# Layer 0 of a two-layer block: normalised rows kept on chip and stored with their routing weights, and slots found as 64 rows by 32 tiles

## The chip, the cores and the metric

The kernel runs on one core of a Trainium2 chip. Its engines are TensorE (PE in the rows; PEld is its weight load), VectorE (DVE), ScalarE (ACT), GpSimd (POOL) and SyncE (SP), which issues most of the DMAs. The metric is the device time of one execution in microseconds; lower is better.

## The reference, cut to what matters

The input is `x` of 16 sequences, 256 tokens, 128 channels: 4096 tokens, 32 tiles of 128. Two layers follow one another, each an attention and a mixture of experts that both read the same normalised rows. Only layer 0 is changed:

```python
xn = layernorm(x)                                   # no weights
q, v, k = split(xn @ Wqvk)                          # 16 heads of 8
w  = softmax(mask(q @ k.T) / sqrt(128))
at = (w @ v) @ Wo
logits = xn @ router_w.T + router_b                 # 8 experts
top_vals, top_ids = top_k(logits, 2); p = softmax(top_vals)
for e in range(8):                                  # capacity 2048 slots: 256 for each expert
    tok, slot = nonzero(top_ids == e, size=256)
    y = (a * (b * sigmoid(b))) @ W_out[e]           # a = xn[tok] @ W[e], b = xn[tok] @ V[e]
    out[tok] += y * p[tok, slot]
x = x + at + out
```

Here the capacity is 2 * 512 * 2 / 8 = 256, computed from a batch of 2, so that most of the 8192 choices get no slot; a token gets at most two slots.

## The kernel before, in words

Each engine has its own program, and semaphores (`wait_ge`, `then_inc`) join them; the order of work is the order in which each engine's function is written. There is no scheduler.

**First stage (0 to 70 us).** For each sequence b, `normalise0` (ACT) writes normalised rows into `xn_ring` (4 buffers), `transposes0` and `products0` (PE) make q, k and v, and q and k are split into three bf16 parts, in `parts0` (ACT), `rest0` (DVE), `middle_parts` and `low0` (POOL). `keep_parts` (SP) stores these to DRAM as `qk_parts` (two DMAs, L436 of 64 KB and L438 of 512 KB), from a ring `qk_p` of 4 buffers, and `load_half` (L451) brings them back stacked as `q_st` and `k_st`, rows by head. `keep_xn` (L456) stores the normalised rows, 128 KB for a sequence, in `x_rows`; the experts gather from there later. At the end SP waits until all parts are stored (L481), and only then moves the first row maxima (`move_max`, L486) into `q_st`.

**The 64 groups (70 to 343 us).** A group is 4 heads of one sequence. In `slot(g)` every engine does its part for group g and its neighbours: PE makes the scores of group g + 3 for the maxima and those of group g again, transposed (`scores`), DVE takes row maxima of group g + 2 (`row_max_late` L1221, `row_max_early` L1214), PE turns them (L1649), ACT negates them, SP moves them, ACT takes the exponential of group g (L874), POOL cuts it off above the diagonal (`cut_off`, L683), PE multiplies with v (`weigh`), and DVE divides (`divide`, L1307 and L1309). The buffer `probs` of the exponentials lies over the first stage's `qk_p` and `xn_ring`.

**Routing, woven into the slots.** In slots 0 to 4 the two best experts are found (`mark_best`, `pick_first`, `weigh_best`, `choose`). At slot `COUNT` = 5 matmuls count what is ahead of each choice. `weigh_experts` (slot 7) computes the two weights and splits them into three bf16 parts; POOL's `place_choices` runs in slot 6; `index_in` (slot 8) makes `row` and `tile_of` of each of the 64 x 128 choices. `mark_tiles` (DVE, slot 9, L1154) writes `in_tile`, and POOL's ten calls (L655, slots 10 to 19) multiply it by token numbers and weights into `of_tile`. `mark_rows` (L1160) compares 128 places with a row, 64 times, in slots 9 to 19, into `of_row`, which lies in `y_top`. `find_slots` (slot 20, L1763) is 64 matmuls of `of_row` by `of_tile` into 128 rows by 5 x 16 columns: token number and weight of each slot. `index_out` makes the indices, POOL gathers the rows in slots 24 to 31 (`collect`, L671, 16 indirect DMAs of 128 rows), and after slot 31 the experts run (`middle`), whose results go back in slots 32 to 39 (`give_back`).

## Time and profile before

| | us |
|---|---|
| median of 3 executions | 843.76 |
| lowest, highest | 843.05, 848.58 |
| the profiled execution, its own time | 841.65 |
| its span | 839.9 |
| first stage, until the first exponential | 70.47 |
| groups 0 to 19 (exponential of 0 to that of 20) | 83.57 |

All rows below are of the profiled execution, whose own time is 2.1 us under the median; its span leaves 1.75 us of it out. The three executions differ by 0.7 us but for one, which lies 5 us higher.

### The profile page before, as it was taken

The numbers are of one execution on the slowest core, as the hardware profiler recorded it, in microseconds if no ns is written. First come the engines' busy times: TensorE is split into PE (matmuls) and PEld (weight loads), VectorE is DVE, ScalarE is ACT, GpSimd is POOL, SyncE is SP. The second block draws the span as 40 slices with busy tenths as digits, with TensorE's granted clock in tenths as the row PEclk, the third lists the DMA queues.
The fourth block names the chain that finished last, engine by engine and source line by source line (L and its number), as shares of the span: only waits on it lengthen the run. The fifth ranks groups of instructions, "written<-read, shape, count | busy, mean of one in ns | idle before, by whom it ended". The sixth has DMA issues, their size and how long they took to land.

```text
span 839.9 us, 17776 instructions
## 1 busy us (share of the span) xinstructions
PE 729.9 (87%) x6148; PEld 539.8 (64%) x6148; DVE 560.2 (67%) x1107; ACT 417.8 (50%) x797; POOL 314.0 (37%) x408
## 2 busy tenths in 40 slices
PE   4658767858977999687889699999999999999997
PEld 3533434525844555486666478888888888888886
DVE  5857888734534888476898477666666666656665
ACT  5634445535434777684767344444444444444442
POOL 2663555452132577401768537121212121211211
PEclk9986899989987999998999899999999999999999
DMA  5993454122011443100112063121212121111100
GB/s 186 274 265 122 143 171 145 54 62 70 15 42 54 139 123 115 52 1 14 53 52 63 27 168 79 51 63 50 59 41 62 50 62 40 65 45 62 51 14 12
DMA packets 66083, 67.58 MB, mean 80 GB/s; under 512 B 6880, under 2 KB 44256, under 8 KB 66016
## 3 DMA queue, kind: packets, MB, share of 16 engines
q1 hardware_dynamic: 64272, 64.32, 25.8%
q0 software_dynamic: 1024, 2.10, 0.9%
q8 instruction: 42, 0.69, 0.3%
q10 hardware_dynamic: 720, 0.27, 0.1%
q14 instruction: 25, 0.20, 0.1%
HBM read 47.51 MB, written 19.01 MB: 79 GB/s over the span
## 4 chain that ended last, share of the span: by engine, by line
PE 67%; DVE 9%; issue 6%; POOL 6%; ACT 5%; DMA 3%; another core or an unknown queue 2%; SPq 1%; ACTq 0%; POOLq 0%; DVEq 0%
PE ps L1741 23%; PE ps L1966 21%; PE ps L1854 3%; DVE m L1221 2%; PE ps L1666 2%; DMA qk_parts<-qk_p 2%; ACT probs L874 2%; POOL probs L683 2%; PE ps L1559 2%; POOL x L666 2%; DVE y_top L1160 1%; PE ps L1809 1%; PE ps L1875 1%; PE ps L1577 1%
## 5 line engine op out<-in xcount | busy, mean ns | idle before, releaser
L1441 DVE SCALAR_TENSOR_TENSOR f_l<-ps,f_h 128x512 fp32r<-128x512 f32 x256 | 176.1, 691 | 114.5 <-ACT f_h L956 113.3
L956 ACT ACTIVATE f_h<-ps 128x512 fp32r<-128x512 f32 x256 | 153.0, 598 | 197.4 <-PE ps L1741 197.4
L1741 PE MATMUL ps<-x_hl,w_h 128*128 (+1 forms) x512 | 201.3, 393 | 0.0
L782 POOL TENSOR_TENSOR acc<-acc,yt 128x512 f32<-128x512 f32 x55 | 70.9, 1289 | 249.8 <-DVE yt L1479 249.8
L874 ACT ACTIVATE probs<-ps 128x1536 f32<-128x1536 f32 x64 | 92.9, 1451 | 47.9 <-PE ps L1586 40.3
L1741 PEld LDWEIGHTS ps<-x_hl,w_h 128*128 128x128 f32 x512 | 96.7, 189 | 19.7
L1741 PE MATMUL ps<-x_hl,w_l 128*128 (+1 forms) x256 | 100.1, 391 | 0.0
L1966 PE MATMUL ps<-f_l,w_h 128*128 128x512 f32 x256 | 99.8, 390 | 0.3 <-DVE f_l L1441 0.3
L1966 PE MATMUL ps<-f_h,w_h 128*128 128x512 f32 x256 | 100.0, 391 | 0.0
L1966 PE MATMUL ps<-f_h,w_l 128*128 128x512 f32 x256 | 99.8, 390 | 0.0
L1221 DVE TENSOR_REDUCE m<-ps 128x4 f32<-128x1024 f32 x64 | 78.1, 1220 | 19.6 <-PE ps L1577 18.0
L683 POOL TENSOR_SCALAR_AFFINE_SELECT probs<-probs 128x512 f32<-128x512 f32 x96 | 59.3, 642 | 71.4 <-ACT probs L874 71.4
L842 ACT ACTIVATE m_neg<-ps 8x128 bf16<-8x128 f32 x64 | 17.1, 267 | 77.5 <-PE ps L1649 60.7
L1966 PEld LDWEIGHTS ps<-f_l,w_h 128*128 128x128 f32 x256 | 48.1, 188 | 11.0 <-DVE f_l L1441 1.0
L1966 PEld LDWEIGHTS ps<-f_h,w_l 128*128 128x128 f32 x256 | 48.2, 188 | 10.0
L1966 PEld LDWEIGHTS ps<-f_h,w_h 128*128 128x128 f32 x256 | 48.2, 188 | 10.0
L1741 PEld LDWEIGHTS ps<-x_hl,w_l 128*128 128x128 f32 x256 | 48.4, 189 | 9.6
L1573 PE MATMUL ps<-k_st,q_st 48*128 48x128 bf16 x256 | 38.1, 233 | 14.7 <-remote 12.5
L1559 PE MATMUL ps<-mask_qk,ident_h 128*128 128x256 bf16 x128 | 28.0, 305 | 25.9 <-DVE m L1221 19.4
L1307 DVE RECIPROCAL rden<-ps 128x8 f32<-128x8 f32 x64 | 13.3, 208 | 55.5 <-PE ps L1774 33.8
L1214 DVE TENSOR_REDUCE m<-ps 128x4 f32<-128x512 f32 x64 | 43.6, 681 | 5.2 <-remote 2.8
L1666 PE MATMUL ps<-probs,v_ring 128*16 128x256 f32 x512 | 43.9, 416 | 1.0 <-ACT wvn L854 1.0
(230 smaller groups left out, 1415.8 us busy)
## 6 DMA issues: line engine op xcount, KB each, us to landing
gate_b<-gate_rows SPq DMA_DIRECT2D x64, 256.0 KB, 3.2
qk_parts<-qk_p SPq DMA_DIRECT2D x16, 512.0 KB, 3.8
k_st<-qk_parts SPq DMA_DIRECT2D x64, 96.0 KB
q_st<-qk_parts SPq DMA_DIRECT2D x64, 96.0 KB
y_tok<-zero SPq DMA_DIRECT2D x8, 512.0 KB, 3.0
w_raw<-in_w_e SPq DMA_DIRECT2D x16, 256.0 KB, 2.8
x_rows<-xn_ring SPq DMA_DIRECT2D x16, 128.0 KB, 3.4
w_up<-in_w_up SPq DMA_DIRECT2D x8, 256.0 KB, 2.8
```

The costliest lines, as they stand in the source:

```text
L683: nc.gpsimd.affine_select(tiles, tiles, pattern=[[0, GH], [1, P]], compare_op=ALU.is_ge, fill=0.0, base=0, channel_multiplier=-1)\
L782: nc.gpsimd.tensor_tensor(acc[:, :], acc[:, :], yt[:, e % 2, :], ALU.add).then_inc(summed, 1)
L874: nc.scalar.activation(probs[:, at(g, HELD), :, :], ps[:, 3:6, :], ACT.Exp, scale=float(D) ** -0.5)\
L956: nc.scalar.activation(r32(f_h[:, m % 4, :]), ps[:, m % 4, :], ACT.Relu).then_inc(f_hi, 1)
L1214: nc.vector.tensor_reduce(m8[:, at(g, 2), :, 0], ps[:, first, :].rearrange("p (h k) -> p h k", h=GH), AX.X, ALU.max).then_inc(early_max, 1)
L1221: nc.vector.tensor_reduce(m8[:, at(g, 2), :, 1], ps[:, first + 1:first + 3, :].rearrange("p c (h k) -> p (c h) k", h=2), AX.X, ALU.max).th ...
L1441: nc.vector.scalar_tensor_tensor(out=r32(f_l[:, m % 4, :]), in0=ps[:, m % 4, :], scalar=0.0, in1=f_h[:, m % 4, :], op0=ALU.max, op1=ALU.su ...
L1559: nc.tensor.matmul(scores_at(g)(c).rearrange("p (h k) -> p h k", h=2)[:, :, P:S], ident_h[:, :], mask_qk[:, :].unsqueeze(1).broadcast_to([ ...
L1573: return nc.tensor.matmul(scores_at(g)(0)[:, h * P:(h + 1) * P], qs[:, 0:P], ks[:, 0:P], start=False, stop=True, skip_group_check=True)
L1666: nc.tensor.matmul(ps_o[32 * h:32 * h + 2 * HD0, :], v_ring[:, u, 0, k * GH + h, :], probs[:, at(g, HELD), 1 + h // 2, h % 2 * S:(h % 2 + ...
L1741: last = nc.tensor.matmul(dst, r32(lhs[i]), r32(rhs[j]), start=(k == 0), stop=(k == 2))
L1966: last = nc.tensor.matmul(ps[:, 4 + e % 2, :], r32(w[i]), r32(fs[:, m % 4, :]), start=(c == 0 and k == 0), stop=(c == FC - 1 and k == 2))
```

## The change

The rows are normalised into `xn_rows`, which holds all 32 tiles with two more columns each (`XW` = 130), in place of the ring, and takes the place of `y_more`. `weigh_experts` writes the two weights of a token into these columns, in slot 6; `keep_xn` then stores the rows in slots 9 to 16, in 8 DMAs of 260 KB; the clears of `y_tok` move from slots 10 to 17 to 17 to 24. The gathered row brings both weights, and `take_weights` (DVE, in `middle`) picks one by `which`. So the bf16 split of the weights and their six POOL calls fall away.

A slot's place is now 64 rows by 32 tiles: `of_row` is made by 8 instructions of 8 x 64 columns, `in_tile` has 2048 columns, POOL makes `of_tile` in 4 calls of 1024 elements (slots 10 to 13), `find_slots` multiplies 64 columns by 64, and its result is taken in two halves. Routing runs a slot earlier (`COUNT` = 4), and `place_choices` is parted over slots 5 and 6.

In the first stage SP holds back the third and fourth part of `x` until the four weights are in; `rb0` moves to SP's queue; ACT loads its table for the square root ahead of the first moments; PE's loop over sequences is written out. PE starts the first scores when sequence 14 is through instead of 15, SP moves the first maxima without waiting for the stores, and ACT waits for the stores ahead of the first exponential.

```diff
@@ -39,7 +39,7 @@
-COUNT = 5
+COUNT = 4
@@ -51,6 +51,10 @@
+SLOT_ROWS = 64
+SLOT_TILES = SLOTS // SLOT_ROWS
+XW = D + 2
+LATE_IN = 12
...
@@ -134,15 +138,17 @@
-        found = sb("found", [P, 5, ST], where=era)
-        pick_p = sb("pick_p", [P, 2, NT], where=era)
-        r_rest = sb("r_rest", [P, 2 * NT], where=era)
-        p_parts = sb("p_parts", [P, 3, 2 * NT], BF16, where=era)
+        found = sb("found", [P, 2, ST], where=era)
+        which = sb("which", [P, 2, ST], where=era)
+        p_both = sb("p_both", [P, 2, ST], where=era)
...
-        y_more = sb("y_more", [P, NT, D], where=era)
-        xg = y_more[:, 0:ST, :]
-        xgT = y_more[:, ST:NT, :].rearrange("p t c -> p (t c)")
-        y_sb = xg
+        xn_rows = sb("xn_rows", [P, NT, XW], where=era)
+        xn_flat = xn_rows.rearrange("p t c -> p (t c)")
+        pick_p = xn_rows[:, :, D:XW].rearrange("p t c -> p c t")
+        y_more = xn_flat[:, 0:NT * D].rearrange("p (t c) -> p t c", c=D)
+        xg = xn_rows[:, 0:ST, :]
+        xgT = xn_flat[:, ST * XW:ST * XW + SLOTS]
+        y_sb = y_more[:, 0:ST, :]
...
@@ -423,9 +423,11 @@
         def _(sp):
             for c, part_in in enumerate(x_in):
+                if c == 2:
+                    sp.wait_ge(w_in, 4 * 16)
...
-            for dst, name in ((tables[:, :, :], "tables"), (rank_e[:, :, :], "rank_e"), (places[:, :], "places"), (w_o[:, :], "w_o"),
+            for dst, name in ((rb0[:, :], "rb0"), (tables[:, :, :], "tables"), (rank_e[:, :, :], "rank_e"), (places[:, :], "places"), (w_o[:, :], "w_o"),
@@ -437,6 +439,10 @@
+            def wait_stored(b):
...
+                sp.wait_ge(qk_stored[b % 4], 32 * (b // 4 + 2))
@@ -450,17 +456,15 @@
-            def keep_xn(b, v):
...
-                sp.wait_ge(xn_ready, (b + 1) * TB)
-                sp.dma_start(x_rows[ds(b * S, S)].rearrange("(t p) d -> p t d", p=P), xn_ring[:, v, :, :]).then_inc(kept[v], 16)
+            def keep_xn(k):
...
+                some = NT // 8
+                sp.dma_start(x_rows[ds(k * some * P, some * P)].rearrange("(t p) d -> p t d", p=P), xn_rows[:, k * some:(k + 1) * some, :])\
+                  .then_inc(rows_out, 16)
...
             for u in range(2):
...
-            for b in range(3):
-                keep_xn(b, b)
@@ -468,17 +472,13 @@
             def keep0(b, v):
-                if more(b, 3):
-                    keep_xn(b + 3, (v + 3) % 4)
...
                 for n in range(16):
                     if STACKS + n * 3 // 4 == b:
-                        sp.wait_ge(qk_stored[n // 8], 64)
+                        wait_stored(n // 8)
...
             for b in range(B):
...
-            for v in range(4):
-                sp.wait_ge(qk_stored[v], 32 * (B // 4 + 1))
@@ -508,10 +508,15 @@
                 if known(g) and 0 <= num(g) - 2 < E:
...
-                if known(g) and num(g) == E + 2:
+                if num(g) == E + 1:
+                    sp.wait_ge(weights_here, 1)
+                    sp.wait_ge(xn_ready, NT)
+                if 0 <= num(g) - E - 1 < 8:
+                    keep_xn(num(g) - E - 1)
+                if num(g) == 2 * E + 1:
...
-                if known(g) and 0 <= num(g) - E - 2 < CLEARS:
-                    clear(num(g) - E - 2)
+                if 0 <= num(g) - 2 * E - 1 < CLEARS:
+                    clear(num(g) - 2 * E - 1)
...
@@ -606,6 +613,13 @@
+            def add_router_bias():
...
+                pool.wait_ge(late_in, LATE_IN * 16)
+                pool.wait_ge(v_put, B + CREDIT)
+                nc.gpsimd.tensor_tensor(logits0[:, :, :], v_all[:, :, H0, :], rb0[:, :].unsqueeze(1).broadcast_to(by_expert), ALU.add).then_inc(route_p, 1)
+            add_router_bias()
@@ -614,14 +628,8 @@
-            pool.wait_ge(v_put, B + CREDIT)
             for u in range(2):
...
-            def add_router_bias():
...
-                pool.wait_ge(w_in, 5 * 16)
-                nc.gpsimd.tensor_tensor(logits0[:, :, :], v_all[:, :, H0, :], rb0[:, :].unsqueeze(1).broadcast_to(by_expert), ALU.add).then_inc(route_p, 1)
@@ -634,12 +642,15 @@
-            def place_choices():
+            def rank_choices():
...
+            def place_choices():
@@ -650,9 +661,8 @@
-                what = (places[:, P + 2 * NT:].broadcast_to([P, NT]), places[:, P + some.start:P + some.stop],
-                        p_parts[:, 0, some], p_parts[:, 1, some], p_parts[:, 2, some])[n // 2]
-                nc.gpsimd.tensor_tensor(of_tile[:, some, n // 2, :], in_tile[:, some, :], what.unsqueeze(2).broadcast_to([P, NT, ST]), ALU.mult)\
+                what = (places[:, P + 2 * NT:].broadcast_to([P, NT]), places[:, P + some.start:P + some.stop])[n // 2]
+                nc.gpsimd.tensor_tensor(of_tile[:, some, n // 2, :], in_tile[:, some, :], what.unsqueeze(2).broadcast_to([P, NT, SLOT_TILES]), ALU.mult)\
...
@@ -702,8 +714,8 @@
                 if known(g) and num(g) == COLLECTS:
-                    pool.wait_ge(indexed, 2)
-                    wait_kept(pool, 1)
+                    pool.wait_ge(indexed, 1)
+                    pool.wait_ge(rows_out, 8 * 16)
...
@@ -807,7 +819,7 @@
                 for t in range(TB):
...
-                    nc.scalar.activation(xn_ring[:, v, t, :], x[:, ds(b * TB + t, 1), :].rearrange("p o c -> p (o c)"), ACT.Identity,
+                    nc.scalar.activation(xn_rows[:, b * TB + t, 0:D], x[:, b * TB + t, :], ACT.Identity,
@@ -821,11 +833,9 @@
                 if more(b, 3):
-                    if not isinstance(b, int) or b >= 1:
-                        act.wait_ge(tr_done, b)
-                        act.wait_ge(kept[(v + 3) % 4], filled(b + 3, (v + 3) % 4, 16))
...
+            nc.scalar.activation(warm[:, :], eps[:, :], ACT.Sqrt)
@@ -853,10 +863,11 @@
-            wait_kept(act, 1)
-            act.wait_ge(qk_lo, B + CREDIT)
             for n in range(2):
...
+            act.wait_ge(qk_lo, B + CREDIT)
+            for v in range(4):
+                act.wait_ge(qk_stored[v], 32 * (B // 4 + 1))
@@ -904,6 +915,8 @@
             def put_down(e):
+                if e == 0:
+                    act.wait_ge(weighted, 3)
...
@@ -1140,34 +1153,39 @@
-            place, expert, row, tile_of, second = (r_s[:, k, :, :] for k in (3, 4, 5, 6, 7))
+            place, expert, row, tile_of, quarter = (r_s[:, k, :, :] for k in (3, 4, 5, 6, 7))
...
-                then(nc.vector.tensor_scalar(second, place, P - 0.5, None, ALU.is_gt))
-                nc.vector.scalar_tensor_tensor(out=row, in0=second, scalar=float(-P), in1=place, op0=ALU.mult, op1=ALU.add)
-                then(nc.vector.scalar_tensor_tensor(out=tile_of, in0=expert, scalar=float(CAP // P), in1=second, op0=ALU.mult, op1=ALU.add))
+                then(nc.vector.tensor_scalar(quarter, place, SLOT_ROWS - 0.5, None, ALU.is_gt))
+                for k in range(2, CAP // SLOT_ROWS):
+                    then(nc.vector.scalar_tensor_tensor(out=quarter, in0=place, scalar=k * SLOT_ROWS - 0.5, in1=quarter, op0=ALU.is_gt, op1=ALU.add))
+                nc.vector.scalar_tensor_tensor(out=row, in0=quarter, scalar=float(-SLOT_ROWS), in1=place, op0=ALU.mult, op1=ALU.add)
+                then(nc.vector.scalar_tensor_tensor(out=tile_of, in0=expert, scalar=float(CAP // SLOT_ROWS), in1=quarter, op0=ALU.mult, op1=ALU.add))
...
             def mark_tiles():
-                nc.vector.tensor_tensor(in_tile[:, :, :], tile_of.rearrange("p c t -> p (c t)").unsqueeze(2).broadcast_to([P, 2 * NT, ST]),
-                                        places[:, 0:ST].unsqueeze(1).broadcast_to([P, 2 * NT, ST]), ALU.is_equal).then_inc(tiles_marked, 1)
+                nc.vector.tensor_tensor(in_tile[:, :, :], tile_of.rearrange("p c t -> p (c t)").unsqueeze(2).broadcast_to([P, 2 * NT, SLOT_TILES]),
+                                        places[:, 0:SLOT_TILES].unsqueeze(1).broadcast_to([P, 2 * NT, SLOT_TILES]), ALU.is_equal).then_inc(tiles_marked, 1)
...
             def mark_rows(n):
...
-                for m in range(n * 2 * NT // MARKS, (n + 1) * 2 * NT // MARKS):
-                    nc.vector.tensor_scalar(of_row[:, m, :], places_h[:, :], row.rearrange("p c t -> p (c t)")[:, m:m + 1], None, ALU.is_equal)\
-                        .then_inc(rows_marked, 1)
+                some = slice(n * 2 * NT // MARKS, (n + 1) * 2 * NT // MARKS)
+                shape = [P, 2 * NT // MARKS, SLOT_ROWS]
+                nc.vector.tensor_tensor(of_row[:, some, :], row.rearrange("p c t -> p (c t)")[:, some].unsqueeze(2).broadcast_to(shape),
+                                        places[:, 0:SLOT_ROWS].unsqueeze(1).broadcast_to(shape), ALU.is_equal).then_inc(rows_marked, 1)
...
             def take_slots():
...
-                nc.vector.tensor_copy(found[:, :, :].rearrange("p u c -> p (u c)"), ps_slots).then_inc(slots_put, 1)
+                for half in range(2):
+                    rows = slice(half * SLOT_ROWS, (half + 1) * SLOT_ROWS)
+                    nc.vector.tensor_copy(found[rows, :, :], ps_slots.rearrange("p (u c k) -> p u c k", u=2, k=2)[:, :, :, half]).then_inc(slots_put, 1)
...
             def index_out():
...
-                dve.wait_ge(slots_put, 1)
+                dve.wait_ge(slots_put, 2)
@@ -1175,22 +1193,23 @@
-            def index_weights():
-                then(nc.vector.tensor_tensor(p_slot[:, :], found[:, 2, :], found[:, 3, :], ALU.add))
-                nc.vector.tensor_tensor(p_slot[:, :], p_slot[:, :], found[:, 4, :], ALU.add).then_inc(indexed, 1)
+                nc.vector.tensor_scalar(which[:, 0, :], whole, N + 0.5, None, ALU.is_lt)
+                then(nc.vector.tensor_scalar(which[:, 1, :], whole, N + 0.5, None, ALU.is_gt))
...
+            def take_weights():
...
+                dve.wait_ge(expert_rows, ST * 16)
+                nc.vector.tensor_tensor(p_both[:, 0, :], xg[:, :, D], which[:, 0, :], ALU.mult).then_inc(weighted, 1)
+                nc.vector.tensor_tensor(p_both[:, 1, :], xg[:, :, D + 1], which[:, 1, :], ALU.mult).then_inc(weighted, 1)
+                dve.wait_ge(weighted, 2)
+                nc.vector.tensor_tensor(p_slot[:, :], p_both[:, 0, :], p_both[:, 1, :], ALU.add).then_inc(weighted, 1)
...
-                then(nc.vector.tensor_tensor(pick_p[:, 1, :], r_s[:, 1, 0, :], pick_p[:, 0, :], ALU.mult))
-                whole, rest = pick_p.rearrange("p c t -> p (c t)"), r_rest[:, :]
-                then(nc.vector.tensor_copy(p_parts[:, 0, :], whole))
-                then(nc.vector.tensor_tensor(rest, whole, p_parts[:, 0, :], ALU.subtract))
-                then(nc.vector.tensor_copy(p_parts[:, 1, :], rest))
-                then(nc.vector.tensor_tensor(p_parts[:, 2, :], rest, p_parts[:, 1, :], ALU.subtract))
+                nc.vector.tensor_tensor(pick_p[:, 1, :], r_s[:, 1, 0, :], pick_p[:, 0, :], ALU.mult).then_inc(weights_here, 1)
...
@@ -1318,6 +1336,7 @@
             def middle():
...
+                take_weights()
...
@@ -1527,13 +1546,13 @@
                 if more(b, 2):
...
-            pe.wait_ge(w_in, 5 * 16)
+            pe.wait_ge(w_in, 4 * 16)
...
-            run_sequences(pe, products0)
+            for b in range(B):
+                products0(b, b % 4)
...
-            pe.wait_ge(qk_res, B + CREDIT)
-            pe.wait_ge(v_put, B + CREDIT)
+            pe.wait_ge(qk_res, B - 1 + CREDIT)
@@ -1677,12 +1696,14 @@
             def count():
...
-                pe.wait_ge(wv_put, COUNT - 4)
...
             for n in range(3):
+                if n == 1:
+                    pe.wait_ge(qk_res, B + CREDIT)
+                    pe.wait_ge(v_put, B + CREDIT)
...
@@ -1757,8 +1778,8 @@
             def find_slots():
...
-                pe.wait_ge(rows_marked, 2 * NT)
-                pe.wait_ge(tiles_known, 10)
+                pe.wait_ge(rows_marked, MARKS)
+                pe.wait_ge(tiles_known, 4)
...
```

On SP, late in the first stage, from sequence 10 to sequence 11, before (`k_st` and `q_st` are the stacked halves, `x_rows` the store of normalised rows):

```order
L451 DMA k_st<-qk_parts 48x1x1024
L451 DMA q_st<-qk_parts 48x1x1024
L456 DMA x_rows<-xn_ring 128x2x128
L436 DMA qk_parts<-qk_p 128x256
L438 DMA qk_parts<-qk_p 128x8x256
L451 DMA k_st<-qk_parts 48x1x1024
```

In every round such a store of rows stands ahead of the two stores of parts. Now, at the same place:

```order
L457 DMA k_st<-qk_parts 48x1x1024
L457 DMA q_st<-qk_parts 48x1x1024
L438 DMA qk_parts<-qk_p 128x256
L440 DMA qk_parts<-qk_p 128x8x256
L457 DMA k_st<-qk_parts 48x1x1024
```

The store of rows has moved from between the rounds to slots 9 to 16; the rest keeps its order.

On DVE, at the end of the slot in which the weights are computed, slot 7, before (`pick_p` are the weights, `p_parts` their bf16 parts):

```order
L1186 TENSOR_SCALAR r_s<-r_s 128x32
L1187 RECIPROCAL pick_p<-r_s 128x32
L1188 TENSOR_TENSOR pick_p<-r_s,pick_p 128x32
L1190 CAST p_parts<-pick_p 128x64
L1191 TENSOR_TENSOR r_rest<-pick_p,p_parts 128x64
L1192 CAST p_parts<-r_rest 128x64
L1193 TENSOR_TENSOR p_parts<-r_rest,p_parts 128x64
```

The maximum of the next slot follows behind these. Now, in slot 6 (L1240 and L1233 are that maximum):

```order
L1210 TENSOR_SCALAR r_s<-r_s 128x32
L1211 RECIPROCAL xn_rows<-r_s 128x32
L1212 TENSOR_TENSOR xn_rows<-r_s,xn_rows 128x32
L1240 TENSOR_REDUCE m<-ps 128x4
L1233 TENSOR_REDUCE m<-ps 128x4
```

Four instructions are gone ahead of the maximum, and the rest stands one slot earlier.

On DVE, in slot 9, where the marks begin, before (L1221 and L1214 are maxima, L1307 and L1309 the division):

```order
L1221 TENSOR_REDUCE m<-ps 128x4
L1214 TENSOR_REDUCE m<-ps 128x4
L1307 RECIPROCAL rden<-ps 128x8
L1309 TENSOR_TENSOR wv_tok<-ps,rden 128x2x32
L1154 TENSOR_TENSOR in_tile<-r_s,places 128x1024
L1160 TENSOR_SCALAR y_top<-places_h,r_s 128x128 x8
```

Both kinds of mark stand in one slot there. Now, from the end of slot 8 to the end of slot 9:

```order
L1169 TENSOR_TENSOR in_tile<-r_s,places 128x2048
L1240 TENSOR_REDUCE m<-ps 128x4
L1233 TENSOR_REDUCE m<-ps 128x4
L1325 RECIPROCAL rden<-ps 128x8
L1327 TENSOR_TENSOR wv_tok<-ps,rden 128x2x32
L1176 TENSOR_TENSOR y_top<-r_s,places 128x512
```

The tile marks have moved up a slot and are twice as wide, and one wide instruction stands for eight small ones.

## Rows read from the trace of the kernel before

**Rows 1.** busy time by stretch; columns as its header says

```profile
core 0: us, PE busy (x) PEld busy (x) DVE busy (x) ACT busy (x) POOL busy (x), PEclk, DMA share, GB/s
...
36.00:52.00 16.00, 8.95 (x51) 7.33 (x50) 10.43 (x32) 7.65 (x19) 8.74 (x11) 1.00 0.90 267
...
104.00:154.00 50.00, 37.02 (x519) 21.77 (x517) 42.12 (x114) 22.89 (x40) 25.05 (x38) 0.93 0.42 141
165.00:205.00 40.00, 28.04 (x332) 15.85 (x333) 18.21 (x34) 15.73 (x29) 17.71 (x22) 0.87 0.24 67
```

**Rows 2.** waits, 20 to 68 us: waiter, releaser, total us, times, longest

```profile
ACT qk_p L819 <- DMA qk_parts<-qk_p: 14.7, 10, 3.0
```

**Rows 3.** timeline of the first 12 us: start, us, engine, line

```profile
2.72 0.62 ACTq L799 DMA_DIRECT2D rb<-in_rb  x1
...
6.11 1.28 ACT L803 ACT_TABLE_LOAD   x1 [6.11 <-DVE mom L1044]
...
10.72 1.12 PE L1514 MATMUL ps<-ident,xn_ring 128*128 128x128 f32 x4 [10.72 <-DMA rb<-in_rb]
```

**Rows 4.** timeline of SP's queue: first, fifth and last of 16 L438 stores

```profile
19.73 0.36 SPq L438 DMA_DIRECT2D qk_parts<-qk_p  x1
...
29.56 0.45 SPq L438 DMA_DIRECT2D qk_parts<-qk_p  x1
...
63.76 0.45 SPq L438 DMA_DIRECT2D qk_parts<-qk_p  x1
```

**Rows 5.** chain that ended last, end of the first stage: start, us, what

```profile
63.76 3.71 DMA qk_parts<-qk_p
...
67.63 1.59 DMA q_st<-m_neg
```

**Rows 6.** timeline of ACT: exponentials (L874) of groups 0, 9, 10, 11, 20, 21

```profile
70.47 1.45 ACT L874 ACTIVATE probs<-ps 128x1536 f32<-128x1536 f32 x1 [3.74 <-PE ps L1586]
...
104.75 1.45 ACT L874 ACTIVATE probs<-ps 128x1536 f32<-128x1536 f32 x1 [0.45 <-PE ps L1586]
...
109.89 1.45 ACT L874 ACTIVATE probs<-ps 128x1536 f32<-128x1536 f32 x1 [0.60 <-PE ps L1586]
...
113.37 1.45 ACT L874 ACTIVATE probs<-ps 128x1536 f32<-128x1536 f32 x1 [0.60 <-PE ps L1586]
...
154.04 1.45 ACT L874 ACTIVATE probs<-ps 128x1536 f32<-128x1536 f32 x1 [0.45 <-PE ps L1586]
...
156.82 1.45 ACT L874 ACTIVATE probs<-ps 128x1536 f32<-128x1536 f32 x1 [0.45 <-PE ps L1586]
```

**Rows 7.** groups by line and shape, 76 to 150 us: count, busy us, mean ns

```profile
L1160 DVE TENSOR_SCALAR y_top<-places_h,r_s 128x128 bf16<-128x128 bf16 x64 | 16.5, 327 | 0.0
...
L1559 PE MATMUL ps<-mask_qk,ident_h 128*128 128x256 bf16 x36 | 8.0, 311 | 16.8 <-DVE m L1221 16.8
...
L655 POOL TENSOR_TENSOR of_tile<-in_tile,p_parts 128x512 bf16<-128x512 bf16 x6 | 6.3, 1049 | 0.0
...
L1154 DVE TENSOR_TENSOR in_tile<-r_s,places 128x1024 bf16<-128x1024 f32 x1 | 1.2, 1215 | 0.0
```

**Rows 8.** timeline of DVE and POOL, 90 to 122 us

```profile
91.98 1.28 POOL L645 TENSOR_TENSOR r_a<-picked,rank 128x512 f32<-128x512 f32 x1
...
92.40 0.90 DVE L1188 TENSOR_TENSOR pick_p<-r_s,pick_p 128x32 f32<-128x32 f32 x1
...
93.34 1.20 DVE L1190 CAST p_parts<-pick_p 128x64 bf16<-128x64 f32 x1
...
95.75 0.23 DVE L1193 TENSOR_TENSOR p_parts<-r_rest,p_parts 128x64 bf16<-128x64 f32 x1
...
104.98 1.39 DVE L1160 TENSOR_SCALAR y_top<-places_h,r_s 128x128 bf16<-128x128 bf16 x8
...
112.31 2.51 DVE L1160 TENSOR_SCALAR y_top<-places_h,r_s 128x128 bf16<-128x128 bf16 x8
...
113.08 1.04 POOL L655 TENSOR_TENSOR of_tile<-in_tile,places 128x512 bf16<-128x512 bf16 x1
```

**Rows 9.** timeline of PE at 150 us

```profile
150.06 2.46 PE L1763 MATMUL ps<-of_tile,y_top 128*128 128x80 bf16 x64
```

**Rows 10.** waits, 160 to 206 us: waiter, releaser, total us, times, longest

```profile
PE ps L1573 <- remote: 8.2, 2, 5.8
```

53 lines of the change are left out of this document (26 added, 27 removed).

## The prediction, made before the changed kernel ran

> **What bounds the kernel now.** I read the table of stretches first, then the waits and the chain that ended last, then the queues' timelines. Three stretches are touched. From 36 to 52 us the DMA engines are 90% busy at 267 GB/s while PE, DVE, ACT and POOL all have room [rows 1], and ACT waits 14.7 us in ten waits for a buffer of `qk_p`, that is, for a store to land [rows 2]: the middle of the first stage is bound by DMA. It begins late, since PE starts at 10.72 us when the last, smallest weight load lands, issued at 2.72 [rows 3], and it ends late: the last store of parts is issued at 63.76 and lands 3.71 us later, only then are the first maxima moved (67.63, 1.59 us) [rows 5], and the first exponential starts at 70.47 [rows 6].
>
> From 104 to 154 us DVE is busy for 42.12 of 50 us, PE for 37 [rows 1], and PE's mask waits 16.8 us for the maxima [rows 7]: DVE sets the pace. A group in which DVE makes 4 marks takes 113.37 - 109.89 = 3.48 us, the eleven groups from 9 to 20 take 154.04 - 104.75 = 49.29, and one without marks, 20 to 21, takes 2.78 [rows 6]. From 165 to 205 us no engine is the bound: PE is busy for 28 of 40 us [rows 1], and two waits for an unknown queue, the longer of 5.8 us, stand in the middle of its own scores [rows 10]. The gathers run in that stretch. Layer 1 (from 343 us) is untouched and enters at nothing; only a clock that differs there could move it.
>
> **First stage: start.** The bias load leaves PE's wait, and the table load (1.28 us at 6.11 [rows 3]) moves ahead of the first moments, so the first rows are normalised some 1.3 us sooner. The root, the scale and two rows of 128 columns follow the moments within 1.7 us by my estimate, and PE could start near 7.8, if the weights have landed, which with 1.5 MB of `x` held back they should. That is 2.9 us. The held back parts of `x` now come about 4 us later, and DVE may wait for them ahead of sequence 4; I take 2.4 us, bounds 0 and 2.9.
>
> **First stage: pace.** The first five L438 stores follow each other by (29.56 - 19.73) / 4 = 2.46 us, the last eleven by (63.76 - 29.56) / 11 = 3.11 [rows 4]. In each of the latter the queue carries the parts (64 + 512 KB), on average 4/3 loads of 96 KB and 128 KB of `x_rows`, 0.85 MB, and 0.85 MB at 267 GB/s [rows 1] is 3.2 us: it agrees with 3.11. Without the 0.131 MB of rows it is 0.49 us less, for eleven rounds 5.4 us, as long as DMA stays the bound: the new pace of 2.62 us is still above the 2.46 at which the first rounds were made without DMA's loads. Bounds: 0, if the pace is that of the engines, and 6.4 (13 stores of rows by 0.49).
>
> **First stage: end.** ACT now waits for the last store itself, so the exponential can follow the landing by some 0.4 us (a negation and the sequencer) in place of 70.47 - 67.47 = 3.0. The maxima must be there too: SP moves them right after the last store and one load of halves, some 1.3 us of issue and 1.6 us of landing, 2.9 us, within the store's 3.71. The bias is added ahead of the last `low0` on POOL and holds back the last store by under 1 us, but SP is that far behind there. Gain 2.6, bounds 1.0 and 2.6. Sum of the stage: 2.4 + 5.4 + 2.6 = **10.4 us**.
>
> **Slots 0 to 20: DVE.** (1) The 64 marks cost 16.5 us at 327 ns [rows 7]. Eight of them alone take 1.39 us, 174 each, and 2.51 when a POOL tile multiplication of 1.04 stands in them [rows 8]; so 11.1 us are their own and 5.4 are waits for POOL. (2) The eight new ones are 512 columns, two inputs from SBUF; the nearest row has 1024 columns at 1215 ns [rows 7], so some 0.65 us each, 5.2 together. (3) They too will wait for POOL: a weight product of 32 columns took 0.90 us beside a POOL multiplication of 1.28 [rows 8]. POOL's tile calls are four of 1024 elements, by 1049 ns for 512 [rows 7] 2.1 us each, and three of the four slots have a mark; the other five marks can meet a cut-off. I put 4 us on it, bounds 0 and 4 * 2.1 = 8.4. (4) `in_tile` doubles: plus 1.2. (5) Two instructions more in `index_in`, 0.2 us each with their wait, taken from the small operations near it: plus 0.5. (6) The split of the weights ran from 93.34 to 95.98: minus 2.6 [rows 8]. (7) `find_slots` is 64 matmuls in 2.46 us with PE's next work behind it [rows 9]; 64 columns for 80 give 0.4 back. Sum: -16.5 + 5.2 + 4 + 1.2 + 0.5 - 2.6 - 0.4 = **-8.6 us**. The two copies of `take_slots`, one more and the same size together, and two comparisons in `index_out`, against the two sums of `index_weights`, cancel.
>
> What is late next: a floor of 2.78 us a group [rows 6]. Eleven groups at the floor would be 30.6, and the forecast leaves about 40 for them, so it isn't reached. POOL's work in slots 10 to 13 is 1.3 (cut-offs) + 2.1 a slot, 3.4, the pace of a slot with a mark; `weigh` comes two slots later and covers it. In all POOL does less, 8.4 us against 10.5.
>
> The Trainium skill, GPSIMD Engine Reference, section Specifications, says that GpSimd shares its SBUF interfaces with VectorE, in contention with VectorE instructions "with two SBUF inputs", too. That speaks against the new form: leaving the fast one-input form doesn't free the marks of POOL. The row on the weight product agrees, so it changes no term here; without contention the sum would be 4 us better.
>
> **What moves at no cost.** `keep_xn` issues in slots 9 to 16 ahead of the pair loads on SP; it stands behind `move_max`, so only later maxima could wait for it. DMA is busy for 42% there [rows 1], and the clears leave these slots. 2.1 MB at 267 GB/s is 8 us of queue in some 27. If SP had no room, each of the eight issues would cost its 0.5 us, 4 us. ACT's new wait stands ahead of the third negation and everything of slot 0; both were behind the stores anyway. `take_weights` is three instructions of 16 columns while DVE waits for the first expert; the wait of ACT's first `put_down` is behind them by two products: nothing, and under 1 us without that cover.
>
> **Sum.** Of its own 841.65 us the profiled execution would keep 841.65 - 10.4 - 8.6 = 822.6; the median of the runs lies 2.1 above it: **825 us**.
>
> **Rivals.** (A) The first stage isn't bound by DMA but by issue and buffers, and keeps 3.11 us a round: 5.4 us come back, 830. For it: POOL and DVE work on 55 to 65% of the time there. Against it: the sum of the bytes fits the pace. 12%.
>
> (B) Gathers and stores of rows of 520 bytes are dearer than of 512 and lengthen PE's waits for the unknown queue. The 40 us from 165 to 205 [rows 1] hold some eight groups, which at 3.4 us would take 27; a half more of the 13 above gives 6.5, 832, and doubling them 838. 10%. The Trainium skill, DMA: Bandwidth & Descriptors, section How a descriptor splits into AXI transactions, says that a piece that doesn't start on a multiple of 256 bytes costs an additional transaction, and rows of 520 bytes start there almost never; no row of this trace has such a size.
>
> (C) Slower than before: SP's queue. If the store of a slot (2080 bytes a partition, cut in four rows) backs up in the DMA queues so that `move_max` of the next slot lands late, every one of the eight slots waits for the exponential. It decides the sign when a slot is lengthened by 19.0 / 8 = 2.4 us; at the landing of a 512 KB store, 3.71 us [rows 5], fully in the path, it is 8 * 3.71 = 29.7, 855. Against it: DMA has half its time free there, and maxima are moved two groups ahead. 3%.
>
> (D) More is gained: marks meet POOL seldom (4 us), groups with marks run as one block at 3.1 us, and the waits of [rows 10] (8.2 us) shrink because PE meets the gathers at other places: 825 - 4 - 6 = 815. 15%.
>
> (E) Half of the change fails: no gain at the start and the end of the first stage (5.0 us), because the late `x` holds DVE and the maxima land after the store: 830. 5%.
>
> The forecast itself has 55%.
>
> **How the numbers follow.** A measurement of this kernel can tell about 1%, 8.4 us, from no change; its own three runs are 0.6% apart at most from the median. Faster by over 1% is under 835.3: the forecast (53 of 55), D (15), A (11 of 12), B (7 of 10, up to a half more) and E (5): 0.91. Within 1%: 0.06. Slower: 0.03. The unknown costs reach from +10 (no pace, all POOL waits at 8.4) to -10; A and most of B stay under 835, D 815. The range of 813 to 835 leaves C, the ends of B and of D out, under 2 in 10.
>
> **What the new profile would show.** PE's first transpose near 8 us; L440 stores 2.6 us apart and the last one near 56; the first exponential near 60; from exponential 9 to 20 about 40 us, with eight `y_top` rows of 0.6 to 1.5; no `p_parts`. The prediction is wrong if stores keep 3.1 us, if marks take over 2 us each, if SP waits for nothing in slots 9 to 16, or if groups 24 to 31 take over 45 us.

## The result, and the profile after

Where no chip is named, "before" is the profile that stands ahead of the prediction. The changed kernel takes **819.75 us** (median of 4 runs, 817.53 to 821.02), the kernel before 843.4 in the same series (839.53 to 848.58): ratio **0.9713, 95% interval 0.9655 to 0.9771**. The forecast was 825, range 813 to 835. The profiled execution took 821.02, with a span of 819.3, against 839.9 before.

The stages are read from the exponentials in ACT's timeline. This is the changed kernel, groups 0, 9 and 20 (it answers to [rows 6]):

```profile
59.74 1.45 ACT L885 ACTIVATE probs<-ps 128x1536 f32<-128x1536 f32 x1 [1.09 <-PE ps L1605]
...
94.41 1.45 ACT L885 ACTIVATE probs<-ps 128x1536 f32<-128x1536 f32 x1 [0.45 <-PE ps L1605]
...
134.48 1.45 ACT L885 ACTIVATE probs<-ps 128x1536 f32<-128x1536 f32 x1 [0.45 <-PE ps L1605]
```

The first exponential comes 10.7 us sooner; groups 0 to 9 take 34.7 us (34.3 before), groups 9 to 20 take 40.07 (49.29). The first stage (10.73) and the slots to 20 (8.83) hold 19.6 of the 20.6 us by which the span is shorter. From exponential 20 to 63 the changed kernel gains 2.80 more (184.78 in place of 187.58). Behind exponential 63, in code that the change doesn't touch, it loses 1.76 (500.04 in place of 498.28): in the first 50 us there TensorE's granted clock is 0.90 in place of 0.95, and the same work keeps it busy for 39.62 in place of 38.01 us.

Two stretches as tables of busy time, with the columns of [rows 1] and to be held against it:

```profile
36.00:52.00 16.00, 11.50 (x70) 8.43 (x70) 11.28 (x31) 9.58 (x22) 11.72 (x14) 1.00 0.99 299
94.41:134.48 40.07, 33.74 (x503) 20.02 (x504) 33.34 (x57) 22.61 (x38) 23.85 (x32) 1.00 0.59 163
```

From 36 to 52 us DMA moves 299 GB/s at a busy share of 0.99, where it moved 267 at 0.90: the DMA engines that I had called full were not. In groups 9 to 20 DVE is still busy for 83% of the time, PE for 84%.

In the waits from 16 to 60 us (they answer to [rows 2]) ACT's wait for stores has shrunk from 14.7 us, which is what it was in this window too:

```profile
ACT qk_p L831 <- DMA qk_parts<-qk_p: 8.5, 10, 2.3
```

In the timeline TensorE starts 3.36 us sooner than in [rows 3], released by the normalised rows and no longer by a load:

```profile
7.36 1.37 PE L1533 MATMUL ps<-ident,xn_rows 128*128 128x128 f32 x4 [7.36 <-ACT xn_rows L822]
```

The fifth store of parts in SP's timeline, against [rows 4]:

```profile
27.20 0.37 SPq L440 DMA_DIRECT2D qk_parts<-qk_p  x1
```

The chain that ended last, at the end of the first stage (start, us, what), against [rows 5]; its first line is the last store's issue:

```profile
54.30 0.43 SPq L440
54.77 0.75 SPq L457
55.57 2.92 DMA q_st<-m_neg
```

The last eleven stores follow each other by (54.30 - 27.20) / 11 = 2.46 us, where it was 3.11. After the last store, SP issues one load of halves and then the move of the first maxima; that move, no longer the store, releases the scores, and the exponential starts 1.25 us after it has landed (58.49 to 59.74). Before, those 1.25 us stood there too (69.22 to 70.47).

The groups by line and shape, 80 to 165 us, against [rows 7]:

```profile
L1176 DVE TENSOR_TENSOR y_top<-r_s,places 128x512 bf16<-128x512 f32 x8 | 9.0, 1127 | 0.0
...
L1169 DVE TENSOR_TENSOR in_tile<-r_s,places 128x2048 bf16<-128x2048 f32 x1 | 2.3, 2281 | 0.0
```

And one mark in the timelines of DVE and POOL, against the first, undisturbed one:

```profile
93.55 0.68 DVE L1176 TENSOR_TENSOR y_top<-r_s,places 128x512 bf16<-128x512 f32 x1
...
97.23 2.34 DVE L1176 TENSOR_TENSOR y_top<-r_s,places 128x512 bf16<-128x512 f32 x1
```

```profile
97.12 1.90 POOL L665 TENSOR_TENSOR of_tile<-in_tile,places 128x1024 bf16<-128x1024 bf16 x1
```

The second mark starts 0.11 us behind a tile multiplication of POOL and ends only 0.55 us after it.

### The profile page after: what moved, and what is told of

Same layout as the page of the kernel before. It is cut to its first block, busy times and chain, and to the rows that moved or that the text cites. A ratio compares the mean times of both kernels' runs of the same rounds, so it can differ in the third digit from the quotient of the medians.

```text
span 819.3 us, 17686 instructions
## 1 busy us (share of the span) xinstructions
PE 727.7 (89%) x6148; PEld 541.0 (66%) x6148; DVE 552.3 (67%) x1053; ACT 418.2 (51%) x798; POOL 312.6 (38%) x402
## 3 DMA queue, kind: packets, MB, share of 16 engines
q0 software_dynamic: 1024, 2.12, 1.0%
## 4 chain that ended last, share of the span: by engine, by line
PE 69%; DVE 9%; POOL 7%; issue 5%; ACT 5%; another core or an unknown queue 3%; DMA 2%; SPq 1%; ACTq 0%; POOLq 0%; DVEq 0%
PE ps L1762 24%; PE ps L1987 21%; PE ps L1875 3%; DVE m L1240 3%; POOL probs L693 2%; POOL x L676 2%; PE ps L1685 2%; PE ps L1578 2%; PE ps L1830 2%; PE ps L1896 1%; ACT probs L885 1%; PE ps L1592 1%; PE ps L1795 1%; PE ps L1596 1%
## 5 line engine op out<-in xcount | busy, mean ns | idle before, releaser
L1240 DVE TENSOR_REDUCE m<-ps 128x4 f32<-128x1024 f32 x64 | 78.0, 1219 | 16.3 <-PE ps L1596 14.6
L1233 DVE TENSOR_REDUCE m<-ps 128x4 f32<-128x512 f32 x64 | 43.6, 681 | 3.4 <-remote 2.3
L1409 DVE TENSOR_TENSOR sc<-ps,upto 128x1024 f32<-128x1024 f32 x32 | 37.7, 1216 | 8.4 <-PE ps L1875 8.2
```

The lines of the kernel that those rows point to most:

```text
L1233: nc.vector.tensor_reduce(m8[:, at(g, 2), :, 0], ps[:, first, :].rearrange("p (h k) -> p h k", h=GH), AX.X, ALU.max).then_inc(early_max, 1)
L1240: nc.vector.tensor_reduce(m8[:, at(g, 2), :, 1], ps[:, first + 1:first + 3, :].rearrange("p c (h k) -> p (c h) k", h=2), AX.X, ALU.max).th ...
L1409: nc.vector.tensor_tensor(sc[:, i % 3, :, 0:2 * P].rearrange("p h (j t) -> p h j t", t=P), diagonal(i % 2), upto[:, :].unsqueeze(1).unsque ...
```

## The experiments

The twelve kernels below ran on three chips. Rows stored, small stores, SP waits for all stores and first stage undone ran on one (the kernel before has a median of 818.61 there); the two kernels again, old start and marks apart on another (818.59). Both are some 25 us faster than the first chip; "the faster chip" below is the second of them, on which both kernels have a profile. The last four ran on a third, as slow as the first (842.39). So an experiment of the first group and the changed kernel are compared across two chips of equal speed. The times are starts of exponentials (e0 is group 0's), the stretches between groups, and what follows exponential 63 to the end of the span, in us. The time is a median of four executions where a ratio stands beside it, and of one elsewhere.

| kernel | e0 | groups 0-9 | 9-20 | 20-31 | 32-63 | behind 63 | time, ratio to before |
|---|---|---|---|---|---|---|---|
| before, again | 71.10 | 34.10 | 49.25 | 37.33 | 91.88 | 498.18 | 815.48 |
| changed, again | 59.95 | 35.02 | 40.20 | 37.29 | 91.90 | 497.45 | 796.36, 0.9731 (0.9691 to 0.9771) |
| rows stored | 62.70 | 34.27 | 41.40 | 37.29 | 91.89 | 499.15 | 799.69, 0.9764 (0.9708 to 0.9820) |
| small stores | 59.62 | 33.33 | 40.42 | 37.28 | 91.89 | 498.55 | 794.62 |
| SP waits for all stores | 60.62 | 34.78 | 37.63 | 37.40 | 91.88 | 500.38 | 796.25 |
| old start | 62.50 | 35.02 | 40.20 | 37.34 | 91.89 | 497.39 | 798.64 |
| first stage undone | 67.81 | 34.08 | 37.58 | 37.31 | 91.90 | 500.31 | 804.97, 0.9833 (0.9776 to 0.9890) |
| marks apart | 59.02 | 34.84 | 36.80 | 37.29 | 91.91 | 500.19 | 794.13, 0.9700 (0.9658 to 0.9742) |
| undone, with ring wait | 67.24 | 34.07 | 37.59 | 51.75 | 105.23 | 499.65 | 829.14, 0.9853 (0.9777 to 0.9928) |
| narrow marks | 59.10 | 34.87 | 50.10 | 51.47 | 101.69 | 497.66 | 828.88 |
| marks and indices | 59.12 | 29.88 | 39.44 | 52.45 | 104.06 | 498.32 | 816.89, 0.9699 (0.9623 to 0.9775) |
| rows stored twice | 59.53 | 34.86 | 40.34 | 51.43 | 101.66 | 497.56 | 819.14 |

Six profiles with the same first stage (the changed kernel twice, marks apart, narrow marks, marks and indices, rows twice) have e0 between 59.02 and 59.95, mean 59.4: that is the spread against which an e0 is read. The changed kernel on the faster chip is the latest of them; its last eleven stores are 2.53 us apart, those of the other five 2.43 to 2.47.

What follows exponential 63 is the same work in all and takes between 497.4 and 500.4 us. Where it takes 499.6 or more, TensorE's granted clock is 0.90 in the first 50 us of it, and 0.93 to 0.95 elsewhere. So up to 3 us won in the slots may not show in the time: with SP's wait for all stores exponential 63 comes 2.7 us sooner than in the changed kernel, and the times are equal (796.25 and 796.36). A part is therefore judged by its stretch and not by the time. Which level the clock takes there, and why, no run settles.

**Both kernels again, on one chip.**

> The changed kernel once more, timed on the chip on which the kernels of this call run, as a base for them. Theory (the change's gain lies in the first stage and in groups 0 to 20, and the stretches from 150 us on differ from chip to chip in both kernels alike): ratio to the kernel before 0.97 again; first exponential near 59.7, groups 9 to 20 in 40 us or, where the marks fall beside POOL's work, 37.6. Rival (rows of 520 bytes make the gathers slower, rival B of the prediction): groups 20 to 31 are longer than those of the kernel before on the same chip by over 2 us.

> The kernel before once more, for its profile on the same chip as the changed kernel. Theory: first exponential at 70.5, groups 9 to 20 in 49 us, groups 20 to 31 within 1 us of those of the changed kernel on this chip (50.4 where the waits for an unknown queue stand, or 37.3 where they don't), and the same from group 32 on. Rival B: groups 20 to 31 shorter than the changed kernel's by over 2 us.

Groups 20 to 31 and 32 to 63 are equal (37.29 and 37.33, 91.90 and 91.88), with no waits for an unknown queue in either. On the first chip both had them and took 50.4 and 50.7. So the stretch differs between chips, not between kernels, and rival B is out.

**The rows stored in the first stage again**, and the same number of small stores.

```
+ def keep_spare(b):
+     sp.wait_ge(xn_ready, (b + 1) * TB)
+     sp.dma_start(spare[ds(b * S, S)]..., xn_rows[:, b * TB:(b + 1) * TB, 0:D])   # 128 KB
+     sp.dma_start(spare[ds(b * S, 1)], xn_rows[0:1, b * TB, 0:D])                 # or 512 B
```

> The changed kernel, and SP stores the normalised rows of each sequence (128 KB, 16 stores) to a spare tensor in the first stage again, as before the change; nothing reads it. Theory (the middle of the first stage is bound by DMA's bytes): the last eleven stores of queries and keys follow each other 0.13 MB by 299 GB/s = 0.44 us more slowly, 2.9 us in place of 2.46, and the first exponential comes 0.44 * 11 = 4.8 us later than at 59.7, near 64.5 us; by the forecast's term 5.4. Rival (bound by issue and buffers): the bytes cost nothing, the first exponential stays within 1 us of 59.7, or moves by the issues alone, which the run with small stores shows.

> The same 16 further stores of SP at the same places, but of 512 bytes each in place of 128 KB: the issues without the bytes. Theory (bytes): first exponential within 1 us of 59.7. Rival (SP's issues are what the removed stores cost): as late as with the whole rows, near 64 us.

The bytes cost 3.1 us against the small stores on the same chip (2.8 against the changed kernel on the faster chip, 3.3 against the mean of 59.4), the issues nothing measurable (59.62). The table of stretches with the rows stored, 36 to 52 us, shows DMA full:

```profile
36.00:52.00 16.00, 9.94 (x59) 7.78 (x59) 8.77 (x26) 7.28 (x18) 10.03 (x12) 1.00 1.00 300
```

DMA's bytes do bound this stretch, but at 300 GB/s: a round of 0.85 MB takes 2.8 us at that rate by my estimate, and these rounds take (57.46 - 27.05) / 11 = 2.76. Without the rows DMA is still at 0.93 to 0.99 from 36 to 52 us, but it is at 0.71 (first chip) and 0.78 (faster chip) from 52 to 60, and the rounds take 2.46, the pace of the first five stores. So the bytes give 0.3 us a round in place of 0.49, 3.3 in all in place of 5.4.

**SP's wait for all stores.**

```
+ for v in range(4):
+     sp.wait_ge(qk_stored[v], 32 * (B // 4 + 1))
```

> The changed kernel, and SP waits for all stores of queries and keys ahead of the first move of maxima, as before the change. Theory: the move of the first maxima (some 1.6 us) and the issues ahead of it now stand behind the landing of the last store, and the first exponential comes 2.6 us later (between 1.0 and 3.0), near 62.3. In the changed kernel the chain ends with that move and not with the store, so the gain of this part may be smaller: rival, under 1 us, if the last store lands before SP comes to the move in either.

e0 is 1.2 us later than the mean of 59.4, but the stores come faster in this profile (2.42 us apart), which hides a part: from the issue of the last store to e0 it takes 7.14 us (53.48 to 60.62), and 5.24 in the changed kernel, 6.74 before (both on the faster chip). The wait is worth 1.2 to 1.9 us. The forecast's 2.6 was too much, since the move of the maxima takes the store's place as the last thing.

**The old start.**

```
- if c == 2: sp.wait_ge(w_in, 4 * 16)              # x held back
- nc.scalar.activation(warm, eps, ACT.Sqrt)        # early load of the table
- pe.wait_ge(w_in, 4 * 16)
+ pe.wait_ge(w_in, 5 * 16)                         # with rb0 last on ACT's queue
```

The order of the loads of `w_q` and `w_k` on ACT's queue goes back with it.

> The changed kernel with the old start alone: x not held back, the bias last on ACT's queue and in TensorE's wait, no early load of the root's table. Theory: TensorE starts at 10.7 us in place of 7.36 and the first exponential comes 2.4 us later than at 59.7 (the prediction's term), at most 3.4, if the whole delay of the start is carried. Rival: with DMA busy for 99% from 36 to 52 us, the loads held back only move bytes, the delay is absorbed and the first exponential stays within 1 us.

TensorE starts at 10.76, released by the load of `rb` again, and e0 is 62.50: 2.6 us later than in the changed kernel on this chip, 3.1 against the mean.

```profile
10.76 1.12 PE L1530 MATMUL ps<-ident,xn_rows 128*128 128x128 f32 x4 [10.76 <-DMA rb<-in_rb]
```

**All of the first stage undone**, then with the ring's wait too.

> The changed kernel with its first stage undone: the rows stored to a spare tensor again, SP's wait for all stores ahead of the first move of maxima, and the old start (x not held back, the bias last on ACT's queue and in TensorE's wait, no early load of the root's table). The slots stay as changed. Theory: the first exponential is back at 70.5 us, 10.7 later than at 59.7, and the time is 820 + 10.7 = 830.5, halfway between both kernels; groups 9 to 20 keep their 40 us. Rival (the first stage's gain partly shifts into or out of the slots, through another clock or DMA state): the first exponential near 70.5 but groups 9 to 20 longer by over 1.5 us, or the time off 830.5 by over 4.

e0 is 67.81, not the 70.5 of the theory nor the 71.1 of the kernel before on the faster chip: the three parts nearly add up (3.3 + 1.2 + 3.1 = 7.6 against 8.4 together, within the spread of e0), and 3.3 us of the first stage's gain were in none of them. They lie in the pace: from the last store to e0 it takes 6.83 us, as before (6.74), but the last eleven stores are 2.80 us apart in place of 3.14. The next kernel put one suspect back:

```
  if more(b, 3):
+     if b >= 1:
+         act.wait_ge(tr_done, b)
+         act.wait_ge(spared[(v + 3) % 4], (b + 3) // 4 * 16)
      normalise0(b + 3, (v + 3) % 4)
```

> The first stage undone as in the run before of that kind (first exponential 67.8 us, against 71.1 of the kernel before on this kind of chip), and in addition ACT's old wait ahead of each normalisation: that the stored rows of the sequence four earlier have landed, as with a ring of four buffers. Theory (the kept rows also free ACT from a wait for a store): the last eleven stores of queries and keys go from 2.80 us a round back to 3.14, the first exponential comes 3.3 us later, at 71.1. Rival 1 (the wait is always met in time, the remainder is the order of the negations): 67.8 within 0.5 us. Rival 2: half of it, near 69.4.

e0 is 67.24: the ring's wait costs nothing, my theory falls. The tables of stretches (36 to 52 us) of the kernel before on the faster chip, and of the undone stage with the ring wait:

```profile
36.00:52.00 16.00, 9.65 (x48) 7.98 (x47) 10.81 (x32) 7.65 (x19) 8.44 (x11) 0.91 0.88 264
```

```profile
36.00:52.00 16.00, 10.19 (x56) 8.43 (x56) 10.95 (x35) 8.34 (x21) 10.25 (x12) 1.00 0.98 299
```

With the same bytes in the same order of issues, the kernel before leaves DMA idle for 12% of the time. In SP's timeline from 30 to 60 us the issues fill 28 of 30 us in either, and an issue of the 128 KB of rows takes 0.94 us in the mean of eight, 0.60 in the undone kernel, with the ring's wait and without it. The source differs (a ring of contiguous rows against rows at a pitch of 520 bytes), and so does its place on chip. Among the parts of the change that no run undid are also PE's loop over the sequences, written out in all kernels but the one before, and the bias, added earlier on POOL. Which of these lengthens the issue, whether the longer issue is the cause or another part is, was not tried: **3.3 us of the 11.2 stay open** (2.7 to 3.9 by the two profiles of either kind).

**The marks away from POOL's tile calls.**

```
- for m in range(MARKS):
-     if MARK - 1 + m * (FIND - MARK + 1) // MARKS == n:
+ for m, at_slot in enumerate((9, 14, 15, 16, 17, 18, 19, 19)):
+     if at_slot == n:
          mark_rows(m)
```

> The changed kernel with its eight wide marks in slots 9, 14, 15, 16, 17, 18, 19 and 19 in place of 9 to 19 evenly, so that none stands in slots 10 to 13, where POOL multiplies the tiles. The marks take 9.0 us in the changed kernel, 0.68 where they run alone. Theory (marks wait for POOL, and TensorE's clock falls behind the long ones): the marks take 6.0 us or less, and groups 9 to 20 come down from 40.1 to 37.0. Rival 1 (no such contention, 40 us is DVE's own work): no mark gets shorter and the stretch stays at 40.1. Rival 2: the marks meet the cut-offs in slots 14 to 19 instead, sum 8 to 9 us, gain under 1 us.

The eight marks take 5.9 us and the stretch 36.80, against 9.0 and 40.20 on the same chip. The clock in it is 1.00 (0.95 in the changed kernel here, but 1.00 on the first chip too, where the stretch took 40.07, so the clock isn't what was won):

```profile
L1176 DVE TENSOR_TENSOR y_top<-r_s,places 128x512 bf16<-128x512 f32 x8 | 5.9, 750 | 0.0
```

Theory held, and the gain of 3.4 is mostly the marks' 3.1 us. The kernels SP waits for all stores and first stage undone say the same without an edit to the marks: by the shift of the phase alone (where DVE's work falls against POOL's) their second and third mark ran in 0.68 to 0.77 us, and groups 9 to 20 took 37.6. In the time little of it arrives, 794.13 against 796.36: behind exponential 63 this kernel takes 2.7 us longer.

**Sixty-four narrow marks.**

```
- nc.vector.tensor_tensor(of_row[:, some, :], row..., places[:, 0:SLOT_ROWS]..., ALU.is_equal)...
+ for m in range(n * 2 * NT // MARKS, (n + 1) * 2 * NT // MARKS):
+     last = nc.vector.tensor_scalar(of_row[:, m, :], places_h[:, 0:SLOT_ROWS], row...[:, m:m + 1], None, ALU.is_equal)
```

> The changed kernel with 64 marks of one bfloat16 input and 64 columns each, eight in a slot, in place of the eight with two fp32 inputs and 512 columns. Theory (an instruction of 64 columns costs nearly as much as one of 128, 174 ns alone in the kernel before, so that the gain of the marks came from their number): between 0.12 and 0.17 us each alone and as much again behind POOL, 10 to 16 us in all against 9.0, and groups 9 to 20 take 41 to 47 us against 40.2. Rival (width decides: half the columns, half the price, and no waits for POOL in the one-input form): under 6 us for the 64 and groups 9 to 20 in 37 us.

```profile
L1175 DVE TENSOR_SCALAR y_top<-places_h,r_s 128x64 bf16<-128x64 bf16 x64 | 18.8, 369 | 0.0
```

Alone, eight take 1.25 us (156 ns each, where those of 128 columns took 174); beside POOL's tile calls eight took 5.71 and 4.44. In all they take 18.8 us, above the theory's 16, and groups 9 to 20 take 50.1, as before the change, and more than the theory's 47. Halving the columns of such a mark saves a tenth; the same 512 columns cost 1.25 us in eight instructions and 0.68 in one wide one. In DVE's timeline the first mark of a slot with a tile call, 64 columns, took this, and the seven behind it 3.74 us together, beside POOL's next operations:

```profile
96.64 1.97 DVE L1175 TENSOR_SCALAR y_top<-places_h,r_s 128x64 bf16<-128x64 bf16 x1
```

**Marks apart and the indices in two slots.**

```
  if n == COUNT + 3:
      index_in()                         # now the two sums alone
  if n == COUNT + 4:
+     index_quarter()                    # the five small operations
+ if n == COUNT + 5:
      mark_tiles()
...
+ for m, at_slot in enumerate((14, 15, 15, 16, 16, 17, 18, 18)):
```

> The changed kernel with the marks all behind POOL's four tile calls (slots 14, 15, 15, 16, 16, 17, 18, 18) and DVE's indices cut in two: the two sums in slot 7, the five small operations in slot 8, the tile marks in slot 9. Theory: the step from exponential 7 to 8 (7.6 us now, with TensorE waiting 3.5 us for the maxima) falls by some 2 us, since 2 us of small operations leave slot 7; the next slots hold them within DVE's room; together with the marks moved, exponential 0 to 20 takes 70 to 71 us against 75.2 (changed kernel) and 71.6 (marks moved alone). Rival: DVE is as busy in slots 8 and 9 (the kernel's clock is half there), and the 2 us come back in them: 71.6 or more.

In the changed kernel group 7 to 8 takes 7.62 us (82.21 to 89.83 on the faster chip): the seven small operations of `index_in` run from 81.94 to 85.16, the maxima stand behind them, and TensorE idles for 3.55 us; from 86 to 90 us its granted clock is 0.50, the lower of its two levels (1.2 GHz), and two products of 256 columns take 0.61 us together, where they took 0.39 before the gap. The kernel before had as long a step there (7.78), behind the split of the weights: the change took one gap away and put another in its place. The wait in PE's timeline:

```profile
86.48 0.61 PE L1578 MATMUL ps<-mask_qk,ident_h 128*128 128x256 bf16 x2 [3.55 <-DVE m L1240]
```

Cut in two, the step takes 4.41 us and groups 0 to 9 take 29.88 in place of 35.02; 2.6 us come back in 9 to 20 (39.44 against 36.80), into which the tile marks (2.28 us) have moved. So e0 to group 20 is 69.3, against 71.6 (marks apart) and 75.2 (changed), which is better than the 70 to 71 of the theory. By time it is the lowest ratio, 0.9699, but the intervals of this, of marks apart and of the changed kernel overlap; from exponential 20 to 63, where this chip's waits for an unknown queue stand, it takes 190.0 us, and 185.1 in the next kernel on the same chip.

**The rows of the slots stored twice.**

```
+ sp.dma_start(spare[ds(k * some * P, some * P)]..., xn_rows[:, k * some:(k + 1) * some, :])
```

> The changed kernel, and each of the eight stores of rows in slots 9 to 16 is followed on SP by a second one of the same size and source to a spare tensor: 2.1 MB and eight issues more. Theory (they cost nothing, SP and the DMA queues have room there): exponential 9 to 20 within 1 us of 40.2. Rival C of the prediction (the stores hold back the moves of the maxima): each slot longer, 4 us in all by the issues alone (0.5 us each), up to 2.4 us a slot and more.

The stretch as a whole stayed (40.34), but not for the theory's reason. Its first three marks missed POOL (0.68 us each), so it should be held against 37.6 (SP waits for all stores, whose marks ran alike): the doubling costs 2.7 us, by one profile of either. One wait, one DMA of the chain that ended last, and one group of DMA issues (last number: us from issue to landing) of this kernel, 104 to 124 us:

```profile
PE ps L1598 <- DMA q_st<-m_neg: 3.6, 4, 1.3
```

```profile
114.78 7.47 DMA q_st<-m_neg
```

```profile
x_rows<-xn_rows SPq DMA_DIRECT2D x5, 260.0 KB, 6.3
```

and the same issue in the changed kernel, on the faster chip:

```profile
x_rows<-xn_rows SPq DMA_DIRECT2D x5, 260.0 KB, 3.2
```

With DMA busy at 0.98 (0.54 in the changed kernel) the maxima land late, one move 7.47 us after its issue, and PE waits for them: rival C's mechanism exists, and stands one more store per slot away.

## Why the prediction was right

On the faster chip e0 moved by 11.15 us and exponential 0 to 20 by 8.1, on the first by 10.7 and 8.8; forecast 10.4 and 8.6. The first stage's sum is near because its pace gave 1.3 to 1.7 us more than forecast and its end 1.1 to 1.3 less, and it holds a gain of 3.3 us whose cause is open: that much of it is luck.

The time itself lies 5 us under the 825. The forecast for the profiled execution, 822.6, was met within 1.6 (821.02). The rest is the step from the profiled execution to the median: I added 2.1 us for it, and this time the median lies 1.3 below. Two things that the sum has at nothing moved, against each other: groups 20 to 63 gave 2.8 us, and what follows cost 1.8, with a lower clock, the one thing that the prediction had named for it.

**First stage, start.** Forecast 2.4. The fifth store comes 2.36 us sooner on the first chip (29.56 to 27.20) and 2.98 on the faster (29.82 to 26.84); undoing the start alone moves e0 by 2.6 to 3.1. Right, and on the faster chip at its upper bound of 2.9.

**Pace.** Forecast 5.4, all from the rows' bytes; measured 3.11 to 2.46 us a round on the first chip, 7.1 us, and 3.14 to 2.53 on the faster, 6.7. The size was near for a reason that only half holds: the bytes are 2.8 to 3.3, the issues none. The step that failed is "the middle of the first stage is bound by DMA", read from a busy share of 0.90 at 267 GB/s: it could move 300. So the old rounds had a slack that the bytes don't explain, 3.3 us in all. Rival A's engines, issues and buffers may have a part in it, which no run shows: its 16 issues as such cost nothing, and its ring of buffers neither.

**End.** Forecast 2.6, measured 1.2 to 1.9 by the wait alone, and 1.3 to 1.5 between both kernels by the times from the last store to e0. The step that failed is that the moved maxima lie "within the store's 3.71". SP comes to them 1.27 us after the store's issue, as forecast (1.3), but they take 2.92 us to land and not the 1.6 taken from [rows 5]: 4.19, behind the store. With the wait put back, the move is issued after the stores have landed and takes 1.67 again. So the landing of the move is the term that was mis-sized.

**Slots.** The marks (terms 1 to 3) went from 16.5 to 9.0 us: minus 7.5, forecast 16.5 - 5.2 - 4 = 7.3. The 0.65 us of one alone was 0.68, and 3.6 us are waits beside POOL's work. `in_tile` cost 1.1 more, forecast 1.2. **Term (5)** was mis-sized: `index_in` took about 3.2 us where it had taken 1.9, plus 1.3 in place of 0.5. POOL stood still beside its small operations before, and now copies and cuts off beside them: the first comparison takes 0.36 us where it took 0.20. No run took this apart. The split's 2.6 us don't show in groups 0 to 9, which grew by 0.4 to 0.9, because routing runs a slot earlier: the tile marks (2.28 us) stand in slot 8, within these groups, where they stood in slot 9, and 2.3 + 1.3 - 2.6 is 1.0. `find_slots` takes 2.21 us where it took 2.46, 0.25 for the 0.4. What I had not priced is the clock: 0.74 of full speed on average in groups 0 to 9 (0.77 before) and 0.95 in 9 to 20 (0.93) on the faster chip, 0.77 (0.77) and 1.00 (0.93) on the first.

**What moves at no cost.** In the waits of the changed kernel from 94 to 135 us none stands for a move of maxima, so the stores in slots 9 to 16 show no delay; SP waited 10.8 us for the negations there (22.0 before, from 104 to 154). The margin is smaller than I wrote: one more such store a slot uses it up.

**The signs.** PE's first transpose (7.36), the last store (54.30), e0 (59.74) and the stretch (40.07) came as foretold; the stores are 2.46 us apart, not 2.6. Six of the eight marks took 0.68 to 1.10 us, the two beside POOL's tile calls 2.34 and 1.74. Groups 24 to 31 took 36.7 us.

**Rivals.** B: rows of 520 bytes. The Trainium skill, DMA: Bandwidth & Descriptors, section How a descriptor splits into AXI transactions, says that a piece that does not start on a multiple of 256 bytes is fetched from the boundary below, and that the bytes ahead of it still cost beats. In the packet records of the changed kernel (104 to 124 us) packets of 520 bytes last 28 ns in the median, those of 512 bytes in the first stage 27, so that no cost beyond that nanosecond is visible in them. The prediction's additional transaction is what that page's table has for 576 bytes (four in place of three). By my estimate from its rule, 520 bytes take three wherever such a row starts, and an aligned row of 512 takes two, so that it is the size and not the start that adds one here. D's first part (4 us with no waits for POOL) is what marks apart showed, 3.4. E: the start and the end of the first stage both gained. C is the last experiment.
